# Loops in the instruction stream, shared coefficient matmuls and a two-pass closing product in a graph layer on one NeuronCore

## What is computed

```python
xn = layernorm(x)
x = x + gnn(xn) + mix(xn)
# gnn: q, k, v = xn @ w.T + b, each again times a second matrix; 16 heads of 64;
#      softmax(q k^T / 8 + mask from 12288 edges) v; out @ wo.T + bo
# mix: q, k = exp(-(xn @ W + b)**2 / 2); v = xn @ Wv + bv
#      coeff = sum over a head's 64 columns of q*k; (coeff * v) @ Wo + bo
# last: xn2 = layernorm(x); an expert of 8 is picked from its moments;
#       x + xn2 @ base_W.T + base_b + (relu(xn2 @ Wd + bd) @ Wu + bu) @ Wc.T + bc
```

## Time and profile before

| what | value |
|---|---|
| median of three runs | 479.64 us (476.05 to 480.69) |
| the profiled execution, whole | 474.66 us |
| its span | 472.9 us |
| TensorE matmuls busy | 465.9 us, 99% |
| VectorE / ScalarE / GpSimd busy | 342.3 / 262.2 / 157.2 us |
| granted TensorE clock | 1.00, that is 2.4 GHz |

### The profile page before, as it was taken

One profiled execution on the slowest core, in us unless ns is written; L12 is line 12 of the kernel. 1 busy time (PEld: TensorE's weight loads), 2 busy tenths in 40 slices (PEclk: granted clock), 3 DMA queues, 4 the chain that ended last, 5 costly groups with the idle time before them and its releaser, 6 DMA issues.

```text
span 472.9 us, 7361 instructions
## 1 busy us (share of the span) xinstructions
PE 465.9 (99%) x2533; PEld 432.4 (91%) x2533; DVE 342.3 (72%) x796; ACT 262.2 (55%) x429; POOL 157.2 (33%) x176
## 2 busy tenths in 40 slices
PE   7999999999999999999999999999999999999996
PEld 5999999999999888999999999999998888888885
DVE  6979966677626259687978888796966794587294
ACT  3734433333324245788989889897974542163170
POOL 3147677777767741002130202212142000050200
PEclk9999999999999999999999999999999999999999
DMA  8877756655444454577675766766679835210463
GB/s 243 325 230 230 239 195 167 176 182 180 154 152 153 133 200 179 175 226 253 205 232 184 235 192 197 247 180 224 192 240 382 308 115 179 89 46 0 155 247 133
DMA packets 39049, 91.92 MB, mean 194 GB/s; under 512 B 7410, under 2 KB 20306, under 8 KB 38884
## 3 DMA queue, kind: packets, MB, share of 16 engines
q1 hardware_dynamic: 33604, 83.15, 54.0%
q0 software_dynamic: 4832, 7.45, 4.7%
q10 hardware_dynamic: 576, 0.85, 0.5%
HBM read 77.96 MB, written 13.47 MB: 193 GB/s over the span
## 4 chain that ended last, share of the span: by engine, by line
PE 87%; DVE 5%; DMA 3%; ACT 3%; issue 1%; SPq 0%; DVEq 0%; ACTq 0%
PE PS L1278 32%; PE PS L1288 28%; PE PS L1283 16%; PE PS L1416 3%; PE PS L1404 2%; DMA turn<-U 2%; PE PS L1535 2%; PE PS L1346 2%; DMA U<-x 1%; DVE U L1076 1%; DVE w_lo L895 1%; PE PS L1266 1%; ACT U L659 1%; PE PS L1539 1%; ACT w_hi L536 1%
## 5 line engine op out<-in xcount | busy, mean ns | idle before, releaser
L895 DVE TENSOR_TENSOR w_lo<-raw,w_hi 128x1024 fp32r<-128x1024 f32 x86 | 104.4, 1225 | 45.0 <-ACT w_hi L536 45.0
L536 ACT ACTIVATE w_hi<-raw 128x1024 fp32r<-128x1024 f32 x87 | 90.8, 1054 | 68.5 <-PE PS L1288 44.1
L454 POOL DMA_INDIRECT table<-evalue,where x96 | 103.0, 1073 | 45.7 <-issue 25.2
L1283 PE MATMUL PS<-xT_hi,w_lo 128*128 128x384 f32 x320 | 61.9, 334 | 0.0
L1278 PE MATMUL PS<-xT_hi,w_hi 128*128 128x384 f32 x320 | 61.9, 334 | 0.0
L1278 PE MATMUL PS<-xT_lo,w_hi 128*128 128x384 f32 x320 | 61.9, 334 | 0.0
L1278 PEld LDWEIGHTS PS<-xT_lo,w_hi 128*128 128x128 f32 x320 | 56.0, 188 | 0.0
L1278 PEld LDWEIGHTS PS<-xT_hi,w_hi 128*128 128x128 f32 x320 | 56.0, 188 | 0.0
L1283 PEld LDWEIGHTS PS<-xT_hi,w_lo 128*128 128x128 f32 x320 | 56.0, 188 | 0.0
L469 POOL TENSOR_TENSOR T_lo<-U,T_hi 128x384 fp32r<-128x384 f32 x8 | 8.2, 1020 | 97.8 <-ACT T_hi L733 97.8
L1288 PE MATMUL PS<-w_hi,T_hi 128*128 128x512 f32 x144 | 40.0, 391 | 0.0
(11 more groups left out here) (241 smaller groups left out, 817.1 us busy)
## 6 DMA issues: line engine op xcount, KB each, us to landing
raw<-weights SPq DMA_DIRECT2D x84, 512.0 KB, 4.6
turn<-U SPq DMA_DIRECT2D x16, 576.0 KB, 4.0
U<-turn SPq DMA_DIRECT2D x64, 144.0 KB, 2.9
U<-key_dram SPq DMA_DIRECT2D x32, 192.0 KB, 4.1
mask<-weights SPq DMA_DIRECT2D x9, 512.0 KB, 5.1
table<-Q POOLq DMA_DIRECT2D x4, 576.0 KB, 9.5
V<-conv SPq DMA_DIRECT2D x4, 512.0 KB, 5.4
U<-table POOLq DMA_DIRECT2D x3, 576.0 KB, 7.5
```

Of the source, the lines that this page charges most:

```text
L454: pool.indirect_dma_start(tables[g], bass.IndirectOffsetOnAxis(ap=where[:, k:k + 1], axis=0), evalue[:, k:k + 1], None, bounds_check=N * N ...
L536: act.activation(w_hi[slot][:], raw[slot][:], ACT.Copy).then_inc(hi_ready[slot], 1)
L895: dve.tensor_tensor(w_lo[slot][:], raw[slot][:], w_hi[slot][:].bitcast(F32), ALU.subtract).then_inc(lo_ready[slot], 1)
L1283: last = pe.matmul(o, wl, src[0][:, k, :], start=False, stop=(k == KB - 1))
```

## The change

Four parts.

1. Coefficients of four pairs at once. The mixer's columns are permuted on the way in (turned), so that a pair's tile holds 16 columns of each of eight heads, and four pairs together hold these heads whole. The four exponentials are added (feat_sum, on VectorE), and only j = 3 and j = 7 split the sum and run the two coefficient matmuls, with a matrix of ones by 16. The four multiplications follow in a row. The unmultiplied values wait in free columns of V2 (raw_value), and mix_hi and mix_lo run four pairs later, those of j = 4 to 7 behind the last pair.
2. Behind the pairs GpSimd issues x's DMA before that of the biases, both among its last mix_lo, and SP, ScalarE and VectorE move the first four base tiles from output blocks 5 to 8 (6 to 9) to 7 to 10 (8 to 11); SP waits for all mix_lo first.
3. Closing product. h's low part goes into rows 64 to 127 beside the high part (h_main), against a P whose rows 64 to 127 repeat its rows 1 to 63 (aug has the columns twice), in one pass; a second pass (h_side) has high times low, the bias rows and what is left over. The first half runs tile by tile, the second all main and then all side matmuls. One of the six last additions goes to ScalarE and GpSimd, and the stores are issued in another order.
4. Jobs 4 to 31 of the first stage are two loops of TensorE (Fori) over a body of four jobs, run five times and twice; the semaphore counts that they wait for come from a register.

What stands in the engines' programs, where the changed and the old one differ.

TensorE in the first stage, before: jobs 4 and 5 stand one after the other (w_hi and w_lo are the parts of a weight tile, xT those of the normalised x), and so on to job 31.

The core of the diff:

```diff
+        feat_sum = v2_rows[:, :, 0:P]
+        rows_of_three = "p (t n) -> p t n"
+
+        def raw_value(j):
+
+            return v2_rows[:, :, j * P:(j + 1) * P] if j else mix_v.rearrange(rows_of_three, t=NT)
...
-                if b == 5:
-
-                    sp.wait_ge(vs_ready, KB)
                 if b == 7:
 
+                    sp.wait_ge(ml_ready, KB)
                     sp.wait_ge(score_read, KB * 6 + 1)
-                if 5 <= b < 9:
-                    load_weights(*E_USES[(b - 5)], weights[72 + 16 + (b - 5)])
+                if 7 <= b < 11:
+                    load_weights(*E_USES[(b - 7)], weights[72 + 16 + (b - 7)])
...
-            for half in range(2):
+            for half, t, done, count in ((0, 0, y_ready, 1), (0, 2, y_ready, 2), (1, 0, y_ready, 3),
+                                         (0, 1, y_added, 1), (1, 1, y_ready, 4), (1, 2, y_ready, 5)):
                 c = slice(half * HALF, (half + 1) * HALF)
-                for t in range(NT):
-                    sp.wait_ge(y_ready, half * NT + t + 1)
-                    sp.dma_start(out[t * P:(t + 1) * P, c], x_rows[:, t, c]).then_inc(stored, 16)
+                sp.wait_ge(done, count)
+                sp.dma_start(out[t * P:(t + 1) * P, c], x_rows[:, t, c]).then_inc(stored, 16)
...
             for j in range(KB):
-                if j:
+                if j >= GROUP:
                     pool.wait_ge(vs_ready, j)
-                    mix_lo(j - 1)
-                    pool.wait_ge(ml_ready, j)
+                    mix_lo(j - GROUP)
+                    pool.wait_ge(ml_ready, j - GROUP + 1)
                 values(j)
                 if j:
                     pool.wait_ge(vs_ready, j + 1)
                     out_lo(j - 1)
                     pool.wait_ge(ol_ready, j)
-                if j == KB - 1:
+            for j in range(KB - GROUP, KB):
+                mix_lo(j)
+                pool.wait_ge(ml_ready, j + 1)
+                if j == KB - GROUP:
+
+                    pool.wait_ge(pT_ready, KB * 2 - 1)
+                    pool.wait_ge(block_ready, KB * 6)
+                    pool.wait_ge(feat_ready, KB // GROUP)
+                    pool.dma_start(x_rows, x.rearrange("(t p) d -> p t d", p=P)).then_inc(xr_in, 16)
+                if j == KB - GROUP + 1:
                     pool.wait_ge(ql_ready, KB)
                     pool.dma_start(row_bo, rows[0:2, :].partition_broadcast(P)).then_inc(rows_in, 16)
-            mix_lo(KB - 1)
-            pool.wait_ge(ml_ready, KB)
-
-            pool.wait_ge(pT_ready, KB * 2 - 1)
-            pool.wait_ge(block_ready, KB * 6)
-            pool.wait_ge(feat_ready, KB)
-            pool.dma_start(x_rows, x.rearrange("(t p) d -> p t d", p=P)).then_inc(xr_in, 16)
...
+            pool.wait_ge(hT_hi, 1)
+            pool.tensor_copy(h_side[0:R, :], h_main[0:R, :].bitcast(F32)).then_inc(h_copied, 1)
+            pool.wait_ge(h_low_in, 2)
+            pool.memset(h_main[R:R + 1, :].bitcast(F32), 1.0).then_inc(hT_ready, 1)
+
+            pool.wait_ge(y_spilt, 1)
+            pool.tensor_tensor(x_rows[:, 1, 0:HALF], spill, x_rows[:, 1, 0:HALF], ALU.add).then_inc(y_added, 1)
...
                 normalise(1)
+                if j >= GROUP:
+                    mix_hi(j - GROUP)
                 if j:
-                    mix_hi(j - 1)
-
-                    act.wait_ge(feat_ready, j)
+
+                    act.wait_ge(feat_exp, j)
+                if j > 1:
+
+                    act.wait_ge(feat_added, adds(j - 1))
                 square(sq_q, 1, 6, rq)
                 if not last:
                     split_hi(*ahead[2])
                 if j:
                     pv_copy(j - 1, 1)
                 act.wait_ge(sq_summed, j + 1)
-                act.activation(sq_q, sq_q, ACT.Exp, scale=-0.5).then_inc(feat_exp, 1)
-                act.wait_ge(feat_exp, j + 1)
-                act.activation(feat[0], sq_q, ACT.Copy).then_inc(feat_hi, 1)
+                if j == 0:
+
+                    act.wait_ge(vs_ready, 1)
+                if j == GROUP:
+
+                    act.wait_ge(feat_ready, 1)
+                act.activation(sq_q.rearrange(rows_of_three, t=NT) if j % GROUP else feat_sum,
+                               sq_q.rearrange(rows_of_three, t=NT), ACT.Exp, scale=-0.5).then_inc(feat_exp, 1)
                 split_hi(*ahead[3])
+                if j % GROUP == GROUP - 1:
+
+                    act.wait_ge(feat_added, adds(j))
+                    act.activation(feat[0].rearrange(rows_of_three, t=NT), feat_sum, ACT.Copy).then_inc(feat_hi, 1)
                 turned_hi(j, 0)
                 if j:
                     out_hi(j - 1)
...
+            mix_hi(KB - 4)
+            mix_hi(KB - 3)
             split_hi(*C_USES[2])
             split_hi(*C_USES[3])
             pv_copy(KB - 1, 0)
             turned_hi(KB - 1, 1)
+            mix_hi(KB - 2)
+            mix_hi(KB - 1)
...
-                act.activation(pc[0][0:BIAS_ROW, half * HALF:(half + 1) * HALF], PS[0:BIAS_ROW, V_BANKS[half], :],
-                               ACT.Copy).then_inc(pc_hi, 1)
+                c = slice(half * HALF, (half + 1) * HALF)
+                act.activation(pc[0][:, c], PS[:, V_BANKS[half], :], ACT.Copy).then_inc(pc_hi, 1)
+                act.wait_ge(bias_ready, 1)
+                act.wait_ge(pc_hi, half + 1)
+                act.activation(pc[1][SIDE_ROW:SIDE_ROW + 1, c], pc[0][0:1, c].bitcast(F32),
+                               ACT.Copy).then_inc(pc_row, 1)
+
+            act.wait_ge(y_done, 2)
+            act.activation(spill, PS[:, E_BANKS[0][1], :], ACT.Copy).then_inc(y_spilt, 1)
...
-                dve.wait_ge(feat_hi, j + 1)
-                dve.tensor_tensor(feat[1], sq_q, feat[0].bitcast(F32), ALU.subtract).then_inc(feat_ready, 1)
+                if j % GROUP:
+                    dve.wait_ge(feat_exp, j + 1)
+                    if adds(j) > 1:
+                        dve.wait_ge(feat_added, adds(j) - 1)
+                    dve.tensor_tensor(feat_sum, feat_sum, sq_q.rearrange(rows_of_three, t=NT),
+                                      ALU.add).then_inc(feat_added, 1)
                 split_weights(*ahead[3])
+                if j % GROUP == GROUP - 1:
+                    dve.wait_ge(feat_hi, j // GROUP + 1)
+                    high, low = (f.rearrange(rows_of_three, t=NT) for f in feat)
+                    dve.tensor_tensor(low, feat_sum, high.bitcast(F32), ALU.subtract).then_inc(feat_ready, 1)
                 turned_lo(j, 0)
-                dve.wait_ge(coeff_done, j + 1)
-                dve.wait_ge(mixv_ready, j + 2)
-                dve.tensor_tensor(mix_v, PS[:, 0, 0:N], mix_v, ALU.mult).then_inc(mix_ready, 1)
+                if j % GROUP == GROUP - 1:
+                    dve.wait_ge(coeff_done, j // GROUP + 1)
+                    dve.wait_ge(mixv_ready, j + 2)
+                    for i in range(j - GROUP + 1, j + 1):
+                        dve.tensor_tensor(raw_value(i), PS[:, 0, 0:N].rearrange(rows_of_three, t=NT), raw_value(i),
+                                          ALU.mult).then_inc(mix_ready, 1)
...
-                if 6 <= b < 10:
-                    split_weights(*E_USES[b - 6])
+                if 8 <= b < 12:
+                    split_weights(*E_USES[b - 8])
...
+            dve.tensor_tensor(h_main[R:P, :], h_sum[0:R, :], h_main[0:R, :].bitcast(F32), ALU.subtract).then_inc(h_low_in, 1)
+            dve.wait_ge(side_const, 3)
+            dve.tensor_tensor(h_side[SIDE_ROW:SIDE_ROW + 1, :], h_sum[0:1, :], h_main[0:1, :].bitcast(F32),
+                              ALU.subtract).then_inc(h_low_in, 1)
...
+            final_rows(0, 0)
             split_p(1)
-
-            def final_rows(half):
-                c = slice(half * HALF, (half + 1) * HALF)
-                for t in range(NT):
-                    dve.wait_ge(y_done, half * NT + t + 1)
-                    dve.tensor_tensor(x_rows[:, t, c], PS[:, E_BANKS[half][t], :], x_rows[:, t, c],
-                                      ALU.add).then_inc(y_ready, 1)
-
-            final_rows(0)
-            final_rows(1)
+            final_rows(0, 2)
+            for t in range(NT):
+                final_rows(1, t)
...
-            for a in range(2, FIRST):
-                pe.wait_ge(bank_free[a % 4], a // 4 + 1)
-                column_job(*A_USES[a], T0 if a >= 3 * KB else xT, A_BANKS[a % 4])
+            for a in (2, 3):
+                pe.wait_ge(bank_free[a], 1)
+                column_job(*A_USES[a], xT, A_BANKS[a])
+
+            for src, begin, end in ((xT, 1, 3 * KB // 4), (T0, 3 * KB // 4, FIRST // 4)):
+                with pe.Fori(0, end - begin) as i:
+                    for s in range(4):
+                        pe.wait_ge(bank_free[s], i + (begin + 1))
+                        column_job(A_SLOTS[s], i + begin, src, A_BANKS[s])
...
-                    pe.wait_ge(mix_ready, j + 1)
+                    if j % GROUP == 0:
+                        pe.wait_ge(mix_ready, j + 1)
```

(83 more changed lines are left out.)

80 lines of the change are left out of this document (42 added, 38 removed).

## The result

Over 21 runs of each kernel on one chip the changed kernel took 480.43 us (median; 478.23 to 485.96) and the kernel before 475.19 us (473.92 to 480.69). The ratio is 1.0102, with a 95% interval of 1.0083 to 1.0122: slower by 1.0%, where I had forecast 0.996. The profiled execution took 478.77 us, its span 477.0, which is 4.1 us longer than the span of the kernel before.

What follows compares the result with a forecast made beforehand. TensorE's matmuls, busy 465.9 of 472.9 us, were taken as the bound. Terms 2.08 + 0.65 - 0.95 = 1.78 us, taken off the three-run median 479.64, gave 477.9 us (ratio 0.996), range 473.9 to 484.

Steps and rivals of the forecast that it cites:

- The fourth job, tile (0,1), goes to ScalarE and GpSimd: Closing product: GpSimd finishes this tile by e + 3.4, its store precedes the last two; last store asked 0.65 us sooner.
- e: Start of the closing product, 464.85 us in the trace of the kernel before; times at the end count from it.
- (b): Rival, chance 0.18: TensorE runs dry at the first stage's five backward branches, 2.05 us each, 10.2 us, giving 488.1 us.
- rival (a): Chance 0.15: in pair 4 the 1.96 us softmax delay behind the bunched multiplications passes through whole, giving 479.7 us.
- Part 3, closing product: At the end, 1.36 us less TensorE work but VectorE sets the end; gain 0.65 us, between 0 and 1.36.
- Part 1, coefficients: In the pairs, twelve matmuls fewer save 2.08 us; waits of 0.05, 0.45 and 0.45 (together 0.95) leave 1.13 us.
- Part 2, transfers: Behind the pairs, moved DMAs and base tiles win nothing; cost taken as 0, at most 4.1 us for a late tile.
- Part 4, loops: First stage as loops: nothing to win, cost taken as 0, with an upper bound of 20.5 us for five fetches.

Runs made afterwards that it cites:

- c1r: The kernel before with only the two TensorE loops of the first stage added, repeated run: ratio 0.9974 (0.9916 to 1.0031).
- b1r: The kernel before plus a one-column GpSimd memset, unused, waiting for the sixth last addition, repeated run: 483.5 us, ratio 1.0106.
- b2: The kernel before plus a one-column GpSimd memset waiting for the first of the six last additions: ratio 1.0002 (0.9953 to 1.005).

## Why the prediction was wrong, step by step

**The step that failed** is in part 3: "The fourth job, tile (0,1), goes to ScalarE and GpSimd". I priced their copy and addition as work beside other work (GpSimd done by e + 3.4) and took the stores for the end of the program, since they were the end before. The work was priced well: GpSimd was done at 468.31, e + 3.5. What I did not price is what follows the last instruction of an engine. The row that would have told stood in the trace of before, the drain of 10.85 us at 440.1, and I read no queue instruction of the last line. By it: 468.3 + 8.4 + 0.2 = 476.9, against 472.5 for the stores, 4.4 us; measured 477.0, 4.5 us. By my own other terms, e would have been 464.85 - 1.13 = 463.7, GpSimd done at e + 3.4, and the span 463.7 + 3.4 + 8.6 = 475.7 against 472.9: slower by 0.6%. None of my rivals had this mechanism; (b) had the direction, for a reason that did not occur. That the measured 480.43 us lies inside my range, close to rival (a)'s 479.7, is luck: the upper part of the range stood for the loops' branches, and I counted from 479.64 us, the median of three runs, where 21 runs of the kernel before give 475.19. From that the same terms would have given 473.4.

**Part 3, closing product.** Right otherwise: the last addition ended at e + 4.41, predicted e + 4.45. The last store was asked for at e + 5.05, before e + 5.46: 0.41 us gained, predicted 0.65, since SP's last ask now ends 0.64 us behind the last addition, before 0.36, which I had kept.

**Part 1, coefficients.** The 18 matmuls of both parts went (2,515 are left and not 2,514, since the page of before has 2,533 and not my 2,532), and three of the four pairs that I named (1, 2, 5, 6) became shorter by what I said; pair 1 did not. Nearly all of the 2.08 us was then given back elsewhere. The starts of the same work in both traces show how much TensorE is ahead at each point:

| start of | before | after | difference |
|---|---|---|---|
| first job of the loops | 31.30 | 32.10 | +0.80 |
| scores of pair 0 | 184.78 | 185.58 | +0.80 |
| of pair 1 | 203.75 | 204.21 | +0.46 |
| of pair 2 | 225.25 | 225.81 | +0.56 |
| of pair 3 | 246.31 | 246.52 | +0.21 |
| of pair 4 | 267.36 | 267.61 | +0.25 |
| of pair 5 | 288.41 | 288.51 | +0.10 |
| of pair 6 | 309.47 | 309.20 | -0.27 |
| of pair 7 | 330.52 | 329.89 | -0.63 |
| pv(7, 0) | 355.98 | 354.95 | -1.03 |
| output block 2 | 357.05 | 356.41 | -0.64 |
| output block 3 | 362.23 | 362.12 | -0.11 |
| product P (L1535, L1617) | 453.93 | 453.89 | -0.04 |

Read it from the top. (By it the coefficients at 245.87 in rows 5 end pair 2, and not pair 1 as my text has it; the rows repeat in every pair, and no term hangs on the name.) 0.8 us was lost before the first loop, where VectorE waits for the gathered table by a DMA through memory:

```profile
28.07 0.35 DVE L1006 SCALAR_TENSOR_TENSOR U<-U,V,cst 128x128 f32<-128x128 f32 x1 [3.89 <-DMA U<-key_dram]
```

Behind it TensorE's weight load for the low part of job 3 waits 1.19 us, before 0.26. That is not the change's: the same wait took 0.6 us in c1r and 1.1 us in b1r, kernels without the rest of the change, and up to 2.7 us in others. Four of the six pairs that lost their coefficients (0, 2, 5, 6) gain 0.34 to 0.37 us, as predicted (0.35); pair 3, which keeps them, gains none, and pair 1 gives back 0.10. Its scores wait for ScalarE, which reads bank 1 only after a softmax tile and a weight tile:

```profile
205.87 0.19 PEld L1483 LDWEIGHTS PS<-T_hi,q_hi 64*128 64x128 f32 x2 [0.67 <-ACT U L761]
```

Before this wait was 0.18 us; here the matmuls taken away ahead of a wait gained nothing. The four multiplications behind pair 3's coefficients cost a wait at the place I named, the first column job after them, at half the price, 0.22 us for 0.45, so that pair 4 gains 0.15:

```profile
270.62 1.34 PEld L1351 LDWEIGHTS PS<-T_hi,w_hi 128*128 128x128 f32 x8 [0.22 <-DVE V L1174]
```

Rival (a), the softmax delay of 1.96 us passing through, did not occur: pair 4 is 20.90 us long, before 21.05. Pair 7 even gained 0.40 us, of which I had forecast nothing; 0.28 of it is a pause ahead of its third score tile that is no longer there. The four multiplications behind j = 7 cost more than I took. GpSimd's timeline (start, us, operation, idle before):

```profile
352.96 1.02 POOL L495 TENSOR_TENSOR T_lo<-V,T_hi 128x384 fp32r<-128x384 f32 x1 [0.42 <-ACT T_hi L776]
354.27 0.81 POOL L534 DMA_DIRECT2D U<-x  x1 [0.30 <-POOL T_lo L495]
355.10 1.26 POOL L495 TENSOR_TENSOR T_lo<-V,T_hi 128x384 fp32r<-128x384 f32 x1
356.65 0.58 POOL L537 DMA_DIRECT2D Q<-rows  x1 [0.30 <-POOL T_lo L495]
358.26 1.85 POOL L495 TENSOR_TENSOR T_lo<-V,T_hi 128x384 fp32r<-128x384 f32 x1 [1.02 <-ACT T_hi L776]
```

The chain is the one I walked, one subtraction, x's DMA, the next, 1 us earlier than I had it. But the subtractions took 1.26 and 1.85 us and not 1.03, so block 2 waited, as predicted, and block 3 too, which I had at nothing: 0.56 and 0.58 us of weight loads, 1.14 for a predicted 0.45.

```profile
PEld PS L1361 <- POOL T_lo L495: 1.1, 2, 0.6
```

So 1.03 us of lead before block 2 became 0.11 at block 3. TensorE reaches P 0.04 us earlier than before, for a predicted 2.08 - 0.95 = 1.13; 0.80 of the difference is the late table, which has nothing to do with the change, and 0.3 its own.

**Part 2, transfers.** Right: 0. No block behind block 3 waits, block 3 and P are 0.11 and 0.04 us ahead.

**Part 4, loops.** Right: 0. From the first job of the loops to the scores of pair 0, with all seven passes between them, 153.48 us pass in both kernels (184.78 - 31.30 and 185.58 - 32.10). The instruction transfers fell from 20 to 16. The queue rows of line 1446 show seven compare-and-branch instructions of 0.08 to 0.24 us; the first stands at 45.7 us, 3.0 us ahead of the first matmul of the next pass (48.74), so whatever a return costs was covered up to that lead. The Trainium skill, "Runtime: NRT & Kernel Launch", section "Instruction fetch mechanics", has a taken branch stall where its target has left the window; no return in this trace shows a gap, so either the body stayed in it or TensorE's queued work covered the fetch, and no run here tells which. Rival (b) is out.

**The sum.** The profile's terms: 0.04 us gained up to P, 0.41 at the stores, 4.5 lost at the drain, 4.1 us lost in the span. The medians lie 5.2 us apart. The 1.1 us between are not explained; both profiled executions lie below their medians, the one of before by 0.5 and the one after by 1.7.

## What to carry to other kernels

The last instruction of each engine is an edge of the program, and not only the last store: before work is moved to an idle engine near the end, read that engine's drain in the trace and add it to the new end. On GpSimd this left room for work until 8.7 us before the end of the span, and whatever ran later set the end. A matmul removed ahead of a wait can give nothing, as in pair 1 here: add up what is gained only at marks behind the next wait.

## What the runs showed of the hardware that I had not expected

GpSimd's drain at the end of a program took 8.4 us beyond its last instruction, whatever that was: a subtraction of 128x1024 (2.40 us; drain 10.85), an addition of 128x512 (1.28; 9.74), a memset of 1x384 (0.41; 8.85) or of 128x1 (0.10; 8.53). The other engines' drains in the changed kernel were 1.0 to 1.5 us. What GpSimd does in that time no run shows.

A subtraction of 128x384 on GpSimd took 1.01 to 1.03 us at all eight places of the kernel before, and 1.26 to 1.87 us at three places behind the pairs in the changed one, while VectorE was at work on its splits and a turned tile; one of these splits took 1.63 us, where the median of all is 1.22. Since the one before at 354.42 took 1.03 us although a split of VectorE began 0.33 us into it, an overlap alone does not settle it, and no run here isolates the cause.

In b2, a run of a slower batch, TensorE's matmuls thinned out while the granted clock was still 1.00, and the clock of 0.50 came behind that: the lower clock followed the idle matmuls and did not start them.
